# Keys of 16 heads from one dense fp32 projection, in a prologue with another order

## The chip, the cores and the metric

The kernel runs on one core of one Trainium2 chip. The metric is the device time of one execution in microseconds (us). The core's engines are TensorE (PE in the rows, its weight loads PEld), VectorE (DVE), ScalarE (ACT), GpSimd (POOL) and SyncE (SP), which issues all loads and stores.

## What is computed

x is 4 batches of 256 tokens of 128 numbers, and ctx is a context of the same shape. Four layers follow each other; each is a cross-attention to ctx and then a mixture of experts, both gated by tanh and both on normalised x:

```python
for L in range(4):
    x = x + tanh(g_xattn[L]) * xattn[L](layernorm(x), ctx)
    x = x + tanh(g_ffn[L]) * moe[L](layernorm(x))
```

Layer 0's attention is an autocorrelation: the spectra of projected queries and keys are multiplied, the inverse transform gives a correlation for each lag, and the five best lags weigh shifted values. Layers 1 and 3 are softmax attention with 16 heads of 8 numbers. Layer 2 has one shared key and value head and a window of 32. The experts of layer 0 are 40 with 6 chosen for a token, of which 8 only pass their input on.

## The kernel before, in words

All of x stays on chip as eight tiles of 128 tokens. Each engine has its own instruction list, written out in order; semaphores tie them together, and an engine that waits holds up all that stands behind in its list. So the order in the code is the order of the work.

The prologue is what comes before the first experts. SyncE issues every load (x, the constants, the context in three layouts, then all weights, then the ring of expert weights). `autocorrelation` on TensorE transforms the context to frequencies (`dft_tokens`, line 583), projects it to keys (`project`, line 591), makes z and vo (lines 604 and 609, the context times the output and value weights), later transforms and projects normalised x, multiplies back (line 624) and mixes vo with the weights of the lags (lines 631 and 635).

Between these steps stand the keys and values of layers 1 to 3, which depend on ctx alone. There are 23 pieces (`chunks`), a piece being one matmul result of 128 x 512; `KV_AT` sets how many stand at each place. A score has to be nearly fp32 accurate, so each number is split into a high part that the fast fp32r format holds and a rest. Keys are stored for it as stacked rows: for each of four heads in a group 8 rows of high part, 8 of the rest, 8 of the high part again, and 2 rows of the constant 1.0 that carry the row maxima. Before, the weights are laid out in this stacked form (`stacked`), so 16 heads need four pieces of 128 columns for each half of the tokens. Each key piece takes

```python
pe.matmul(o, w[:, 0, :], chi[:, c], start=True, stop=False)
pe.matmul(o, w[:, 0, :], clo[:, c], start=False, stop=False)
mm = pe.matmul(o, w[:, 1, :], chi[:, c], start=False, stop=True)
```

on TensorE (lines 558 to 560), two passes on ScalarE with different signs and scales by row (lines 1025 and 1029), and a sum of the two on GpSimd (line 415), which `stage` holds until it is written to a DRAM buffer (`keys`, line 309). Once all keys are written, `stack_keys` reads them back into kz, the buffer of three batches from which attention takes its weights.

kz has to be zero where no rows are written. GpSimd fills all of it (line 503). The arithmetic of the routing (`route`) and of the experts' first weights comes at the prologue's end: `turn_weights` (line 654) waits for VectorE's routing parts.

## Time and profile before

| | |
|---|---|
| median of 3 runs | 725.25 us |
| lowest, highest | 723.22, 726.19 us |
| the profiled execution, its own time | 724.92 us |
| its span in the profile | 723.1 us |
| TensorE busy, share of the span | 637.2 us, 88% |
| VectorE busy | 526.2 us, 73% |
| ScalarE busy | 379.8 us, 53% |
| GpSimd busy | 266.8 us, 37% |
| mean granted clock of TensorE | 0.962 |

The profile gives each instruction's start and duration, and for each idle stretch the instruction that ended it. Busy shares are means over the whole span; the prologue is its first 100 us. An fp32 matmul stands in the profile as two records, an fp32r matmul as one. The granted clock is 1.00 at 2.4 GHz and 0.50 at 1.2 GHz.

### The profile page before, as it was taken

To read this page: it belongs to the slowest core of one execution; us is meant where nothing else is said; L and a number is where in the kernel's file an instruction comes from. 1 tells how busy PE (TensorE), PEld (TensorE's weight loads), DVE (VectorE), ACT (ScalarE), POOL (GpSimd) and SP (SyncE) were. 2 spreads that over 40 slices of the span, in tenths; PEclk is the share of its full clock that TensorE was granted. 3 is DMA by queue.
4 is the path that set the end of the run, shared out by engine and by line. 5 is a ranking of instruction groups with operands and counts; after the bars stand their busy time and mean duration, and the time that the engine had idled before them with its cause. 6 is when DMAs were issued, how large, how long until landed. Compare 5 with 4: busy or idle time off the path is not lost.

```text
span 723.1 us, 11826 instructions
## 1 busy us (share of the span) xinstructions
PE 637.2 (88%) x3590; PEld 450.3 (62%) x3590; DVE 526.2 (73%) x1290; ACT 379.8 (53%) x652; POOL 266.8 (37%) x463
## 2 busy tenths in 40 slices
PE   2787669998899988998899889999998899987997
PEld 1576537775567655676566546777766677654774
DVE  5473789898787636887864568888877888555886
ACT  1545255543356662543466337777744466632774
POOL 7633355662310121463112115666642100201663
PEclk9998689998999998999999999999999999998999
DMA  8221042111001010011000301111110010000110
GB/s 292 76 90 67 7 152 83 44 40 45 5 3 32 3 32 0 23 44 31 10 5 5 88 0 39 36 44 43 37 37 0 4 33 2 4 1 0 38 44 38
DMA packets 24087, 28.50 MB, mean 39 GB/s; under 512 B 4002, under 2 KB 19938, under 8 KB 24036
## 3 DMA queue, kind: packets, MB, share of 16 engines
q1 hardware_dynamic: 24036, 27.87, 12.3%
q8 instruction: 26, 0.43, 0.2%
q14 instruction: 25, 0.20, 0.1%
HBM read 22.22 MB, written 5.24 MB: 38 GB/s over the span
## 4 chain that ended last, share of the span: by engine, by line
PE 72%; DVE 16%; ACT 5%; issue 4%; POOL 1%; DMA 1%; DVEq 0%; SPq 0%; ACTq 0%; POOLq 0%
PE PS L665 11%; PE PS L666 11%; PE PS L667 11%; PE PS L687 5%; PE PS L891 4%; PE PS L529 4%; PE PS L800 4%; PE PS L874 3%; DVE negmax L1527 2%; DVE consts L1533 2%; PE PS L906 2%; DVE qst L1487 2%; PE PS L871 1%; PE PS L583 1%; PE PS L847 1%
## 5 line engine op out<-in xcount | busy, mean ns | idle before, releaser
L425 POOL TENSOR_TENSOR wpair<-ring,ones_col 128x128 fp32r<-128x128 f32 (+1 forms) x150 | 75.6, 504 | 139.9 <-PE PS L667 96.2
L1432 DVE TENSOR_TENSOR pT<-pT,PS 128x512 f32<-128x512 f32 x150 | 102.4, 684 | 29.3 <-ACT pT L1067 23.5
L1166 ACT ACTIVATE pT<-PS 128x512 f32<-128x512 f32 x160 | 92.0, 592 | 50.1 <-PE PS L874 40.7
L1438 DVE TENSOR_TENSOR hid_lo<-pT,hid_hi 128x512 fp32r<-128x512 f32 x150 | 110.6, 738 | 2.8 <-ACT hid_hi L1074 1.6
L427 POOL TENSOR_TENSOR wpair<-ring,wpair 128x128 fp32r<-128x128 f32 (+1 forms) x150 | 103.2, 688 | 11.7
L1074 ACT ACTIVATE hid_hi<-pT 128x512 fp32r<-128x512 f32 x150 | 93.9, 626 | 14.4 <-DVE pT L1432 13.3
L665 PE MATMUL PS<-hid_hi,wpair 128*128 128x512 f32 x150 | 86.6, 577 | 4.4 <-DVE hid_lo L1438 4.4
L665 PE MATMUL PS<-xhi,wpair 128*128 128x512 f32 x204 | 85.0, 417 | 2.2 <-DVE pT L1432 1.4
L1067 ACT ACTIVATE pT<-PS,ring 128x512 f32<-128x512 f32 x96 | 66.0, 689 | 37.1 <-PE PS L667 37.1
L666 PE MATMUL PS<-xlo,wpair 128*128 128x512 f32 x204 | 82.5, 404 | 0.0
L667 PE MATMUL PS<-xhi,wpair 128*128 128x512 f32 x204 | 82.2, 403 | 0.0
L800 PE MATMUL PS<-kz,qst 128*128 128x256 f32 x256 | 59.0, 314 | 11.5 <-DVE negmax L1533 7.1
L482 POOL CAST nmpart<-negmax 128x8 fp32r<-128x8 f32 x48 | 9.2, 191 | 158.6 <-DVE emask L1540 69.0
L874 PE MATMUL PS<-qst,kz 128*128 128x256 f32 x256 | 65.3, 340 | 2.1 <-ACT pT L1166 2.0
L1533 DVE CUSTOM_DVE_ANT_0 consts<-PS,ctx_tok,negfloor 128x256 bf16<-128x256 f32 x128 | 54.3, 480 | 9.1 <-PE PS L800 8.7
L666 PE MATMUL PS<-hid_lo,wpair 128*128 128x512 f32 x150 | 59.1, 394 | 0.0
L667 PE MATMUL PS<-hid_hi,wpair 128*128 128x512 f32 x150 | 59.1, 394 | 0.0
L1067 ACT ACTIVATE pT<-PS 128x512 f32<-128x512 f32 x54 | 32.0, 597 | 48.9 <-PE PS L667 48.8
L800 PEld LDWEIGHTS PS<-kz,qst 128*128 128x128 f32 x256 | 39.5, 191 | 27.3 <-issue 8.4
L1527 DVE TENSOR_REDUCE negmax<-PS 128x2 f32<-128x512 f32 x64 | 42.8, 689 | 12.5 <-PE PS L800 12.5
L665 PEld LDWEIGHTS PS<-xhi,wpair 128*128 128x128 f32 x204 | 40.2, 197 | 14.4 <-issue 5.0
L874 PEld LDWEIGHTS PS<-qst,kz 128*128 128x128 f32 x256 | 44.7, 194 | 6.9 <-ACT pT L1166 3.0
(242 smaller groups left out, 1252.8 us busy)
## 6 DMA issues: line engine op xcount, KB each, us to landing
ring<-in_mlp SPq DMA_DIRECT2D x48, 128.5 KB, 2.1
ring<-in_glu SPq DMA_DIRECT2D x27, 192.0 KB, 2.4
keys<-qst SPq DMA_DIRECT2D x18, 256.0 KB, 2.0
kz<-keys SPq DMA_DIRECT2D x36, 128.0 KB, 3.1
qst<-kfull SPq DMA_DIRECT2D x96, 4.0 KB
wq<-in_wq SPq DMA_DIRECT2D x3, 256.0 KB, 4.2
consts<-in_consts SPq DMA_DIRECT2D x1, 740.0 KB, 5.0
x_res<-in_x SPq DMA_DIRECT2D x1, 512.0 KB, 3.6
```

The source lines that it names most:

```text
L425: pool.tensor_tensor(wpair[:, pair, 0, c], w, ones, ALU.mult).then_inc(M["wstep"], 1)
L427: pool.tensor_tensor(wpair[:, pair, 1, c], ring[:, slot, c], wpair[:, pair, 0, c].bitcast(f32), ALU.subtract).then_inc(ready, 1)
L665: pe.matmul(o, w_hi, hi, start=start, stop=False, skip_group_check=True)
L666: pe.matmul(o, w_hi, lo, start=False, stop=False, skip_group_check=True)
L667: return pe.matmul(o, w_lo, hi, start=False, stop=start, skip_group_check=True)
L800: mm = pe.matmul(PS[:, v % 2, q * S:(q + 1) * S], qst[:, h // HGRP, b * S + q * P:b * S + (q + 1) * P], keys_of(b, h), start=True, stop=True)
L874: mm = pe.matmul(PS[:, 2 + w % 2, k * S:(k + 1) * S], keys_of(b, h)[:, k * P:(k + 1) * P], qst[:, h // HGRP, b * S:(b + 1) * S], start=(L ...
L1067: act.activation(act_out[:, hf, :], PS[:, 2 + hf, :], func, bias=bias).then_inc(M["act"], 1)
L1074: act.activation(hid_hi[:, kept, :], hid[:, hf, :], ACT.Copy).then_inc(M["hi"], 1)
L1166: act.activation(pT[:, w % 8, :], PS[:, 2 + w % 2, :], ACT.Exp, scale=sc).then_inc(A["p"], 1)
L1432: dve.tensor_tensor(hid[:, hf, :], src[:, hf, :], PS[:, 6 + hf, :], ALU.mult).then_inc(M["hid"], 1)
L1438: dve.tensor_tensor(hid_lo[:, kept, :], hid[:, kept % 2, :], hid_hi[:, kept, :].bitcast(f32), ALU.subtract).then_inc(M["lo"], 1)
```

## The change

The key weights are no longer stacked. A key piece is one fp32 matmul of 128 dense columns, all 16 heads at once (`key_columns` sets their order), for half of the tokens. ScalarE reads the result once and rounds it to fp32r, which is the high part (`key_high`). TensorE then subtracts this high part from the same PSUM bank with a matmul by minus the identity (`key_rest`), and ScalarE reads the rest (`key_low`). Three whole parts per layer are written to DRAM (high, rest, high), and the stacking happens when they are read back, 24 rows instead of 32. The rows of the constant 1.0 are written once, by four small transfers from `ones2` (`flag_keys`). There are 11 pieces instead of 23. GpSimd no longer splits weights or context or sums keys.

The prologue is written in another order. TensorE starts with 14 matmuls on zeros and transforms context and normalised x one behind the other; the correlation follows product by product. VectorE prepares the routing tables ahead of the products. z, vo and layer 1's keys come behind the correlation, the values of layers 1 and 3 behind the mixing, the keys of layers 3 and 2 and layer 2's values behind the first expert's matmuls. The loads come in another order: 640 columns of the constants ahead of ctx_tok, the rest of them later, ctx_nat and ctxT after the small ones. The fill of kz is divided: GpSimd and VectorE fill half of the first batch's place each, ScalarE the other two in eight instructions.

```diff
-        KV_AT = (4, 8, 12, 18)
-        chunks = ([("k", 1, hf, a) for hf in range(NHALF) for a in range(HGRP)]
-                  + [("v", L, hf, 0) for L in (1, 3) for hf in range(NHALF)]
-                  + [("k", 2, hf, 0) for hf in range(NHALF)] + [("v", 2, 0, 0)]
-                  + [("k", 3, hf, a) for hf in range(NHALF) for a in range(HGRP)])
+        chunks = ([("k", 1, 0), ("k", 1, 1)] + [("v", L, hf) for L in (1, 3) for hf in range(NHALF)]
+                  + [("k", 3, 0), ("k", 3, 1), ("k", 2, 0), ("k", 2, 1), ("v", 2, 0)])
+        KV_MIX, KV_LN = 2, 6
...
-            sp.dma_start(consts[:, 0:C_BAND], t["consts"]).then_inc(ld_const, 16)
+            sp.dma_start(consts[:, 0:C_INV], t["consts"][:, 0:C_INV]).then_inc(ld_const, 16)
             sp.dma_start(ctx_tok[:, :, :], t["ctx_tok"]).then_inc(ld_ctx, 16)
...
+            def save_keys(L):
+                sp.wait_ge(kv_out, keys_done[L])
+                for part, rows in enumerate((key_hi[L], key_lo[L], key_hi[L])):
+                    sp.dma_start(kd[L][part, :, :], rows.bitcast(f32)).then_inc(k_saved[L], 16)
...
                     for j in range(HGRP):
-                        rows = slice(32 * j, 32 * j + 32)
+                        rows = slice(32 * j, 32 * j + SROWS)
...
-            pool.memset(kz[:, :, :, :].bitcast(f32), 0.0).then_inc(kz_set, 1)
+            pool.memset(kz[:, 0, 0:H // 2, :].bitcast(f32), 0.0).then_inc(kz_set, 1)
...
                 if kind == "k":
-                    pe.matmul(o, w[:, 0, :], chi[:, c], start=True, stop=False)
-                    pe.matmul(o, w[:, 0, :], clo[:, c], start=False, stop=False)
-                    mm = pe.matmul(o, w[:, 1, :], chi[:, c], start=False, stop=True)
+                    mm = pe.matmul(o[0:wk[L].shape[1], :], wk[L][:, :], ctxT[:, hf * HALF:(hf + 1) * HALF], start=True,
+                                   stop=False, skip_group_check=True)
...
+            def key_rest(n):
+                kind, L, hf = chunks[n]
+                rows = wk[L].shape[1]
+                pe.wait_ge(kv_hi, k_before[n] + 1)
+                pe.matmul(PS[0:rows, 6 + n % 2, :], minus[0:rows, 0:rows], key_hi[L][:, hf * HALF:(hf + 1) * HALF],
+                          start=False, stop=True, skip_group_check=True).then_inc(kv_rest, 1)
...
-                    for c in range(KV_AT[3], len(chunks)):
-                        key_value(c)
+                    for c in (KV_LN, KV_LN + 2):
+                        for half in (c, c + 1):
+                            key_value(half)
+                        for half in (c, c + 1):
+                            key_rest(half)
+                    key_value(len(chunks) - 1)
...
-            pe.wait_ge(set_pool, 3)
-            pe.wait_ge(set_dve, 2)
+            pe.wait_ge(set_pool, 1)
+            keep_busy(7, 14)
             autocorrelation()
...
+            def key_high(n):
+                act.activation(key_hi[L][:, hf * HALF:(hf + 1) * HALF], PS[0:rows, 6 + n % 2, :], ACT.Identity,
+                               bias=consts[0:rows, col:col + 1]).then_inc(kv_hi, 1)
+            def key_low(n):
+                act.wait_ge(kv_rest, k_before[n] + 1)
+                act.activation(key_lo[L][:, hf * HALF:(hf + 1) * HALF], PS[0:rows, 6 + n % 2, :], ACT.Identity,
+                               bias=consts[0:rows, col:col + 1]).then_inc(kv_out, 1)
...
+            def zero_keys(first, last):
+                for c in range(first, last):
+                    act.activation(blocks[:, c, :, :], zerob[:, :].unsqueeze(1).broadcast_to([P, 2, HALF]),
+                                   ACT.Copy).then_inc(kz_set, 1)
...
             def autocorrelation():
+                dve.memset(kz[:, 0, H // 2:H, :].bitcast(f32), 0.0).then_inc(kz_set, 1)
...
+                prepare_routing()
+                for n, (qx, kx) in enumerate(((0, 0), (0, 1), (1, 1), (1, 0))):
+                    dve.wait_ge(ac["kfe"], kx + 1)
+                    dve.wait_ge(ac["qfreq"], qx + 1)
+                    dve.tensor_tensor(prod[:, (0, 3, 1, 2)[n], :], PS[:, 6 + qx, :], kfreq[:, kx, :], ALU.mult).then_inc(ac["prod"], 1)
...
-                prepare_routing()
```

TensorE's list at the kernel's start, before. PS is PSUM, consts the constants with the transform matrix, att_w the weights of layer 0, oT the buffer of z and vo, qst the split context:

```order
L583 MATMUL PS<-consts,ctx_tok 128x256 [waits ld_const,ld_ctx,set_dve,set_pool]
L583 MATMUL PS<-consts,ctx_tok 128x256 x7
L591 MATMUL PS<-att_w,kf 128x128 [waits ld_att0,ac_kine]
L591 MATMUL PS<-att_w,kf 128x128 x7
L604 MATMUL PS<-att_w,kfull 128x128 [waits ld_ctx]
L604 MATMUL PS<-att_w,kfull 128x128 x7
L609 MATMUL PS<-oT,att_w 128x512 [waits ac_ze]
L609 MATMUL PS<-oT,att_w 128x512
L558 MATMUL PS<-qst,hid_hi 128x512 [waits ac_voe,wk_split1,bias_rows,ctx_lo]
...
L583 MATMUL PS<-consts,xn 128x256 [waits ln_xn]
L583 MATMUL PS<-consts,xn 128x256 x7
L591 MATMUL PS<-att_w,kf 128x128 [waits ac_qine]
```

And in the changed kernel, where zerob is a tile of zeros, kf the context's spectrum and oT that of x:

```order
L508 MATMUL PS<-zerob 128x512 [waits set_pool]
L508 MATMUL PS<-zerob 128x512 x13
L567 MATMUL PS<-consts,ctx_tok 128x256 [waits ld_ctx,ld_const]
L567 MATMUL PS<-consts,ctx_tok 128x256 x7
L567 MATMUL PS<-consts,xn 128x256 [waits ln_xn]
L567 MATMUL PS<-consts,xn 128x256 x3
L567 MATMUL PS<-consts,xn 128x256 [waits ln_xn]
L567 MATMUL PS<-consts,xn 128x256 x3
L575 MATMUL PS<-att_w,kf 128x128 [waits ac_kine,ld_att0]
L575 MATMUL PS<-att_w,kf 128x128 x7
L575 MATMUL PS<-att_w,oT 128x128 [waits ac_qine]
```

The transform of x (`xn`) stood behind two projections, vo and four key pieces; it now stands right behind the context's, and the wait for VectorE's constants (`set_dve`) is gone from the first.

VectorE's list before, from its first instructions and around the products of the spectra (line 1302; pT<-PS,qf), with the routing tables (wrpair, b2part) behind them:

```order
L1564 CAST identb<-consts 128x128 [waits ld_const]
L1566 CAST pick<-consts 96x32
...
L1297 COPY kf<-PS 128x512 [waits ac_qin]
L1302 TENSOR_TENSOR pT<-PS,qf 128x512 [waits ac_qfreq,ac_kfe]
L1302 TENSOR_TENSOR pT<-PS,qf 128x512 x3
L1304 TENSOR_TENSOR pT<-pT 128x512 [waits ac_prod]
L1283 CAST wrpair<-wr 128x40 [waits ld_route]
...
L1290 TENSOR_TENSOR b2part<-pT,b2part 96x128 [waits dstep]
L1309 MAX pT<-PS 128x8 [waits ac_corr,dstep]
```

And in the changed kernel:

```order
L1308 MEMSET kz 128x2048
L1248 BN_STATS stats<-x_res 128x6 [waits ld_x]
...
L1325 COPY oT<-PS 128x512 [waits ac_qin]
L1298 CAST wrpair<-wr 128x40 [waits ld_route,bias_rows]
...
L1305 TENSOR_TENSOR b2part<-pT,b2part 96x128 [waits dstep]
L1332 TENSOR_TENSOR pT<-PS,qf 128x512 [waits ac_qfreq,ac_kfe,dstep]
L1332 TENSOR_TENSOR pT<-PS,qf 128x512 [waits ac_qfreq,ac_kfe] x3
L1334 TENSOR_TENSOR pT<-pT 128x512 [waits ac_prod]
L1338 MAX pT<-PS 128x8 [waits ac_corr]
```

The tables stand ahead of the products now, the casts of the constants behind the normalisation (not shown), and each maximum waits for its own batch.

ScalarE's list before, around z and vo (oT) and around the exponential of the lag weights (pT, 128x20):

```order
L1184 ACTIVATE oT<-PS 128x1024 [waits ac_z]
L1186 ACTIVATE oT<-PS 128x1024 [waits ac_vo]
L1188 ACTIVATE gtan<-gates 128x8 [waits ld_gate]
L1025 ACTIVATE qst<-PS,kbs,consts 128x512 [waits vall_set,set_dve,kv_mm]
L1029 ACTIVATE kfull<-PS,kba,consts 128x512
...
L1035 ACTIVATE vall<-PS 128x64x8 [waits kv_mm] x4
L1040 ACTIVATE qf<-pick 96x2048 [waits ac_prod]
L1198 ACTIVATE pT<-pT 128x20 [waits ac_top]
L1025 ACTIVATE qst<-PS,kbs,consts 128x512 [waits k_saved0,kv_mm]
L1029 ACTIVATE kfull<-PS,kba,consts 128x512 [waits k_ready]
```

And in the changed kernel, from the context's projected spectrum (qf) on:

```order
L1195 ACTIVATE qf<-PS 128x512 [waits ac_kfreq] x2
L1197 ACTIVATE oT<-PS 128x1024 [waits ac_z]
L1017 ACTIVATE qst<-PS,consts 128x512 [waits kv_mm,ld_rest]
L1017 ACTIVATE qst<-PS,consts 128x512 [waits kv_mm]
L1202 ACTIVATE pT<-pT 128x20 [waits ac_top]
L1204 ACTIVATE oT<-PS 128x1024 [waits ac_vo]
L1025 ACTIVATE qst<-PS,consts 128x512 [waits kv_rest] x2
L1208 ACTIVATE pT<-PS 128x512 [waits ac_mo]
L1036 ACTIVATE vall<-PS 128x64x8 [waits kv_mm,vall_set]
```

The exponential stood behind the four value pieces and the spreading of picks; it now stands behind the copy of z and two high key parts, which wait for TensorE's key matmuls.

## Rows read from the trace of the kernel before

**Rows 1.** The profile's page, busy time, share of the span and instructions.

```profile
...
PE 637.2 (88%) x3590; PEld 450.3 (62%) x3590; DVE 526.2 (73%) x1290; ACT 379.8 (53%) x652; POOL 266.8 (37%) x463
...
```

**Rows 2.** Chain of waits, 0 to 45 us: start, us, engine, tile and line.

```profile
...
6.34 7.43 DVE pick L1566
...
13.86 6.62 PE PS L583 x16
...
```

**Rows 3.** DMA issues, 0 to 100 us: KB each, us from issue to landing.

```profile
...
ring<-in_glu SPq DMA_DIRECT2D x4, 192.0 KB, 4.7
...
x_res<-in_x SPq DMA_DIRECT2D x1, 512.0 KB, 3.6
ctx_tok<-in_ctx_tok SPq DMA_DIRECT2D x1, 512.0 KB, 5.8
...
kz<-keys SPq DMA_DIRECT2D x1, 128.0 KB, 3.0
...
```

**Rows 4.** SyncE issues in order of time: start, us, how many.

```profile
...
15.76 1.85 SPq L333 DMA_DIRECT2D ring<-in_glu  x4
...
```

**Rows 5.** TensorE in order of time: start, us, line, operation, records.

```profile
...
21.31 2.05 PE L591 MATMUL PS<-att_w,kf 128*128 128x128 f32 x16 [0.85 <-DVE kf L1294]
...
26.26 1.98 PE L609 MATMUL PS<-oT,att_w 128*128 128x512 f32 x4 [1.11 <-ACT oT L1184]
...
45.01 5.34 PE L624 MATMUL PS<-consts,pT 128*128 128x256 f32 x24
...
58.77 5.26 PE L563 MATMUL PS<-wv,ctxT 128*128 128x8 f32 x32 [2.27 <-ACT kfull L1029]
...
70.26 1.99 PE L635 MATMUL PS<-oT,pT 128*128 128x256 f32 x8 [1.59 <-ACT pT L1202]
77.97 2.27 PE L541 MATMUL PS<-consts,xn 128*128 128x128 f32 x8 [5.72 <-DVE xn L1242]
...
83.97 0.77 PE L665 MATMUL PS<-xhi,wpair 128*128 128x512 f32 x1
...
88.69 0.40 PE L558 MATMUL PS<-qst,hid_hi 128*128 128x512 f32 x1
...
```

**Rows 6.** TensorE and others by stretch: busy, then granted clock (PEclk).

```profile
...
80.00:84.00 4.00, 3.68 (x19) 3.47 (x17) 1.11 (x2) 0.60 (x1) 2.69 (x5) 0.50 0.00 0
88.00:95.00 7.00, 5.16 (x19) 2.96 (x17) 6.68 (x31) 5.66 (x11) 3.83 (x3) 1.00 0.14 52
...
```

**Rows 7.** ScalarE in order of time.

```profile
...
25.19 1.02 ACT L1184 ACTIVATE oT<-PS 128x1024 f32<-128x1024 f32 x1 [0.70 <-PE PS L604]
...
41.37 0.78 ACT L1025 ACTIVATE qst<-PS,kbs,consts 128x512 fp32r<-128x512 f32 x1 [2.94 <-PE PS L560]
...
```

**Rows 8.** VectorE in order of time.

```profile
...
40.74 2.48 DVE L1302 TENSOR_TENSOR pT<-PS,qf 128x512 f32<-128x512 f32 x4 [2.21 <-PE PS L591]
...
44.65 2.58 DVE L1283 CAST wrpair<-wr 128x40 fp32r<-128x40 f32 x4
...
51.03 0.43 DVE L1309 MAX8 pT<-PS 128x8 f32<-128x256 f32 x1
...
72.36 0.75 DVE L1276 SCALAR_TENSOR_TENSOR x_res<-PS,gtan,x_res 128x512 f32<-128x512 f32 x1 [10.47 <-PE PS L635]
...
84.18 0.49 DVE L1345 COPY pT<-PS 128x320 f32<-128x320 f32 x1 [2.57 <-PE PS L648]
...
91.16 1.59 DVE L1374 SCALAR_TENSOR_TENSOR pT<-pT 128x320 f32<-128x320 f32 x1
...
98.67 0.90 DVE L1403 TENSOR_TENSOR pT<-pT 128x256 bf16<-128x256 f32 x1
...
```

**Rows 9.** GpSimd (POOL) in order of time.

```profile
...
3.26 10.40 POOL L503 MEMSET kz<- 128x12288 f32 x1
...
42.90 5.46 POOL L415 TENSOR_TENSOR qst<-qst,kfull 128x512 fp32r<-128x512 f32 x4 [5.54 <-ACT kfull L1029]
...
91.12 6.62 POOL L415 TENSOR_TENSOR qst<-qst,kfull 128x512 fp32r<-128x512 f32 x5 [8.28 <-ACT kfull L1029]
...
```

More of the change, by code:

```diff
@@ L131, in build @@
         kz = sb("kz", [P, KSLOTS, H, S], f32r)
-        kd = {L: nc.dram_tensor(f"keys{L}", (P, 1 if L == 2 else HGRP, N), f32, kind="Internal").ap() for L in range(1, 4)}
+        kd = {L: nc.dram_tensor(f"keys{L}", (3, HD if L == 2 else P, N), f32, kind="Internal").ap() for L in range(1, 4)}
         v_cols = {1: NT * H * 9, 2: B * NW * 9, 3: NT * H * 9}
@@ L406, in layer_norm @@
                     pool.tensor_tensor(rstd[:, c], veps[:, c], mhalf[:, c], ALU.pow).then_inc(ln_rstd, 1)
-            def complete_keys(first, last):
-                for n in range(first, last):
-                    kind, L, hf, a = chunks[n]
-                    if kind == "k":
-                        k = k_before[n]
-                        pool.wait_ge(kv_out, n + 1)
-                        pool.tensor_tensor(stage(k), stage(k).bitcast(f32), kfull[:, k % 2, :], ALU.add).then_inc(k_ready, 1)
             def split_weights(L, glu):
@@ L636, in autocorrelation @@
                                    vo[:, b * S:(b + 1) * S], start=True, stop=True)
-                mm.then_inc(ac["out"], 1)
+                    if b % 2 == 1:
+                        mm.then_inc(ac["out"], 1)
+                for n in range(KV_MIX, KV_LN):
+                    key_value(n)
             def route(L, hf):
@@ L1201, in _ @@
+            for n in range(0, KV_MIX):
+                key_low(n)
             act.wait_ge(ac["mo"], 1)
-            act.activation(mixo, PS[:, 2, :], ACT.Copy).then_inc(ac["moe"], 1)
+            act.activation(mixo, PS[:, 0, :], ACT.Copy).then_inc(ac["moe"], 1)
+            act.wait_ge(vall_set, 6)
+            for n in range(KV_MIX, KV_LN):
+                values(n)
             layer_norm(1)
+            spread_picks()
             route(0)
-            for n in range(KV_AT[3], len(chunks)):
-                key_value(n)
+            for c in (KV_LN, KV_LN + 2):
+                for n in (c, c + 1):
+                    key_high(n)
+                for n in (c, c + 1):
+                    key_low(n)
@@ L1207, in _ @@
+            values(len(chunks) - 1)
             experts(0, True)
@@ L1258, in layer_norm @@
                         ln_statistics(s, 0)
[L1259 removed]
+                if s > 0:
                     ln_apply(s, 0)
@@ L1486, in finish_queries @@
                     dve.wait_ge(A["qt"], pre["qt"] + HGRP * hf + a + 1)
-                    dve.scalar_tensor_tensor(out=dst, in0=PS[:, bank, :], scalar=consts[:, C_SGN + 3:C_SGN + 4],
+                    dve.scalar_tensor_tensor(out=dst, in0=PS[:, bank, :], scalar=consts[:, C_SGN + 1:C_SGN + 2],
                                              in1=dst.bitcast(f32), op0=ALU.mult, op1=ALU.add).then_inc(A["qe"], 1)
```

351 lines of the change are left out of this document (163 added, 188 removed).

## The prediction, before the changed kernel was run

> **What bounds the kernel now.** I read the profile's page first: TensorE is busy 88% of the span [rows 1], but that is a mean over four layers and a prologue. The change touches the prologue alone, up to where the first mixture of experts has its routing weights, so I read the chain of waits from 0 us on, and then each engine in order of time there. Seen so, the prologue is a chain of waits rather than of TensorE work, and it ends at 99.6 us (98.67 + 0.90) [rows 8]. Four things make it long.
>
> First, GpSimd's zero fill of kz holds from 3.26 to 13.66 us [rows 9]. VectorE's casts of the constants, issued at 6.3, end at 13.77 [rows 2], just behind it, although consts was there. TensorE waits for them and starts at 13.86. Second, that first transform takes 6.62 us for 16 records of 256 columns, 0.41 each [rows 2]; later the same shape takes 5.34 us for 24, 0.22 each [rows 5]: the first ran at the lower of TensorE's two levels, 1.2 GHz. Third, keys are made in 18 pieces, each with two ScalarE passes (0.78 us, the second 0.67 behind the first) [rows 7] and a GpSimd sum; the query transform, the value pieces and the mixing matmuls stand behind them in the queues. That is why the products of the spectra start at 40.74 and the result is added to x only at 72.36, after 10.47 us in which VectorE idled [rows 8]. Fourth, GpSimd's sums (5.46 us for four, 6.62 for five) [rows 9] lie beside VectorE's small casts and routing arithmetic, which are slow there: four casts of at most 40 columns take 2.58 us, one pass over 320 elements 1.59 [rows 8].
>
> **The new order, step by step.** Times are those of the changed kernel, worked out from the rows.
>
> *Start.* SyncE issues one load per 0.46 us (four in 1.85) [rows 4]. x lands at 4.3, as before (issue 0.7 + 3.6) [rows 3]. ctx_tok landed 5.8 us after its issue at 1.7, behind 740 KB of consts; only 320 KB of it stand ahead now. Between x's landing and its own lay 1,252 KB in 3.1 us, 400 KB per us, so 420 KB less is 1.1 us: it lands at 6.4. But 14 zero matmuls stand ahead of it from 1.3 us on: 0.43 us each at 1.2 GHz (512 columns), 6.0 in all. TensorE starts its first transform at 7.3, not 13.86: 6.5 us gained. I let the clock rise at about 8.5, since in rows 2 it needed all of 6.6 us of work. So the first transform takes 4.1 us (three records at 0.41, 13 at 0.22) and ends at 11.4. x must be normalised by then; from the add at 72.36 to the first transposes at 77.97 [rows 5, 8] such a normalisation takes 5.6 us even with two adds in it, so it is ready by 9.9. Query transform 3.6: 15.0. Then both projections, 2.05 each [rows 5]: 17.1 and 19.1, the first half of the second at 18.1.
>
> *VectorE before the products.* It copies the query spectrum at 15.0 to 15.7 and then prepares the routing tables, which stood behind the products and stand ahead of them now. Before, this took 6.4 us (44.65 to 51.03) [rows 8], the first 3.7 under GpSimd's sums (to 48.36) [rows 9]. GpSimd is now idle until the expert weights land (15.76 + 4.7 = 20.5) [rows 3, 4], so I take 3.2: the uncovered 2.7, and an estimate of 0.5 for the small casts that GpSimd held up. If that cover fails, 3.2 more. Products start at 18.9 instead of 40.74.
>
> *Products to add.* Four products take 2.48 [rows 8]. The twelve correlation matmuls (0.445 each) [rows 5] now follow product by product, so batch 0 is done 4.7 us after the products' start and batch 3 at 6.0. Maxima take 1.0 us a batch (0.43 for the values [rows 8], as much for their places, and a load): 8.7. VectorE then has 0.9 of lag work. ScalarE's exponential stands behind the copy of z (1.02) [rows 7] and two key copies: z's matmuls end at 8.0, the two key matmuls (0.99 each, fp32 of 512 columns) [rows 5] at 10.0, the second copy at 10.8, the exponential at 11.0, so VectorE waits 1.4 us. This is the late thing that comes next. Weights and mixing matrix take 2.1 (13.1), transposes 0.6 (13.7); ScalarE is at the copies of vo and the two low key parts until 14.4, then copies the mixing matrix, 15.0; half of the last product (1.99 for both) [rows 5], 16.0. The add starts at 18.9 + 16.1 = 35.0 instead of 72.36: 37.4 gained. The rest of TensorE's old work here, four value pieces, now lies in the gap in which it idled 5.72 us [rows 5].
>
> *Add to logits.* 11.8 us before (72.36 to 84.18) [rows 8]. The halves are now chained one behind the other; by the same durations I get 11.3, logits at 46.3.
>
> *Routing.* VectorE needed 15.4 us (84.18 to 99.57); without GpSimd's 6.62 us of sums [rows 9] I get 9.8, since the last eight instructions took 8.4 there (91.16 to 99.57) and should take some 2.8, by the 0.49 of an undisturbed pass over 320 elements at 84.18 [rows 8]. But TensorE must get through 12 expert matmuls and all keys of layers 3 and 2 before it turns the weights, and each pair of key halves now goes matmul, ScalarE, matmul, ScalarE, with the bank free only then. At 2.4 GHz: expert matmuls 2.9, keys of layer 3 until 7.1, of layer 2 until 9.95 (its value piece may start), the 32 small records 5.26 as before [rows 5]: 15.2. So this becomes the bound here, and the turn comes at 46.3 + 15.2 = 61.5 instead of 99.6. VectorE's gain of 5 us is lost again.
>
> The sum: 99.6 - 61.5 = 38.1 us. The profiled execution took 724.92 us, so 686.8; the median is 0.3 above it, so 687.
>
> **What I take as nothing.** The zero fill on VectorE (2,048 columns; GpSimd took 0.85 ns per column [rows 9]) lies ahead of x's landing if it runs at once. If GpSimd's fills hold VectorE as they did in rows 2, it ends near 7.3 and moves the products by 1.1. The Trainium skill ("SBUF — State Buffer", Who interferes with whom) says that the port shared by VectorE and GpSimd is held for the whole instruction, and that a VectorE instruction with at most one SBUF input outside the two-port modes does not contend; for the casts the trace agrees (7.43 us behind the fill), for a memset nothing here shows it. By the Trainium skill the term is 0, by the row 1.1.
>
> ScalarE's eight fills of 1,024 columns (1.02 each by [rows 7]) lie in gaps: four before the first spectrum, two and two between copies whose next wait is longer. The ones written by DMA, the keys' way through DRAM (9 saves instead of 18) and the restacking have no reader before layer 1's attention, over 80 us later. Restacking the last batch there and in layer 3 moves 24 rows instead of 32, landing 3.0 before [rows 3]. Layers 1 to 3 otherwise issue the same work.
>
> The Trainium skill ("DMA: Bandwidth & Descriptors", Why a DMA increments its semaphore by 16 and not by 1) speaks against that edit: a transfer is spread over the largest number up to 16 that divides its slowest dimension, so 32 rows use 16 engines and 24 use 12. Its runs of 1 KB are 8 per engine either way, and by that rule the price is 0 too. No row before has 24 rows.
>
> **Rivals.** (1) *The key chain at the lower clock*, 0.14. From 80 to 84 us TensorE was granted half [rows 6], having idled 5.72 us [rows 5], and twelve matmuls from 83.97 to 88.69 took 4.7; after 88 it had full clock. Half clock through the whole chain gives 5.1 + 5.5 + 5.6 + 5.8, about 22 us instead of 15.2: 694. Against it: the value pieces fill that idle stretch now. (2) *TensorE never warms early*, 0.04: every TensorE step up to the add at half rate costs some 16 us more: 703. (3) *The start does not move*, because a load that the first transform needs is late and the order of loads buys nothing; TensorE starts at 13.9 again: 6.6 less gain, 693.5, 0.04. (4) *More than forecast*, 0.05: the clock rises by 6, key halves overlap, the small records at full rate (4.0): 683. (5) *Slower than before*, 0.03: restacking of the last batch in layers 1 and 3. Each must be late by more than 19 us, half of the 38.1, before it decides; at 21 each the kernel is 3.6 slower, 729. That needs a transfer seven times its 3.0 us; nothing speaks for that but the new shape.
>
> **How the numbers follow.** The forecast has 0.70. Its own bounds: -1.2 (small records at full rate), -0.9 (clock), +1.1 (fill), +3.2 (routing tables uncovered), +2.5 (first transforms cold): 684 to 693. With rivals 1, 3 and 4, which hold 0.23, the range is 681 to 697; outside lie rivals 2 and 5 and tails of the rest. A measurement of this kernel can tell about 0.5%, 3.6 us. All but rival 5 and a mishap I don't see are over 28 us off, so 0.95 faster, 0.02 within, 0.03 slower.
>
> **What will show it.** The first transform starts near 7.3 with ctx_tok landed before; the products near 18.9; VectorE waits 1.4 us for ScalarE's exponential; the add at 35; logits at 46; the turn of the weights waits for TensorE's small records and not for VectorE; the routing passes that took 1.59 and 0.90 take under 0.6; from there on all stages are as long as before. Wrong I am if the products wait for the tables by more than 4 us, if the clock is at half past 46, or if layers 1 to 3 change their length.

## The result, and the profile after

The changed kernel takes 689.44 us (median of 4 runs, 687.98 to 691.10); the kernel before took 725.72 on the same chip (4 runs, 723.22 to 727.65). The ratio is 0.950, with a 95% interval of 0.946 to 0.954: 36 us, or 5%, less. The forecast was 687 (681 to 697). The profiled execution took 688.41 us, with a span of 686.6 where before had 723.1.

The milestones of the forecast come first, in the order of time on TensorE and VectorE of the changed kernel (start, us, engine, line, operation, count; in brackets the wait ahead of it). TensorE:

```profile
1.31 6.00 PE L508 MATMUL PS<-zerob 128*128 128x512 bf16 x14 [1.31 <-POOL ones_col L393]
8.02 3.69 PE L567 MATMUL PS<-consts,ctx_tok 128*128 128x256 f32 x16 [0.71 <-DMA ctx_tok<-in_ctx_tok]
11.55 3.62 PE L567 MATMUL PS<-consts,xn 128*128 128x256 f32 x16
...
46.73 0.77 PE L657 MATMUL PS<-xhi,wpair 128*128 128x512 f32 x1
...
51.72 1.88 PE L531 MATMUL PS<-ctxT,wk 128*128 128x512 f32 x4
...
58.18 3.88 PE L535 MATMUL PS<-wv,ctxT 128*128 128x8 f32 x32 [0.18 <-ACT kfull L1025]
61.91 1.07 PE L646 MATMUL PS<-identb,pT 128*96 128x128 bf16 x8
```

VectorE of the same kernel:

```profile
1.23 1.76 DVE L1308 MEMSET kz<- 128x2048 f32 x1 [1.23 <-PEq L1722]
...
15.89 0.42 DVE L1298 CAST wrpair<-wr 128x40 fp32r<-128x40 f32 x4
...
19.17 2.48 DVE L1332 TENSOR_TENSOR pT<-PS,qf 128x512 f32<-128x512 f32 x4
...
24.17 0.43 DVE L1338 MAX8 pT<-PS 128x8 f32<-128x256 f32 x1 [1.34 <-PE PS L596]
...
29.86 0.17 DVE L1351 TENSOR_REDUCE pT<-pT 128x4 f32<-128x20 f32 x1 [0.78 <-ACT pT L1202]
...
34.66 0.75 DVE L1291 SCALAR_TENSOR_TENSOR x_res<-PS,gtan,x_res 128x512 f32<-128x512 f32 x1 [2.64 <-PE PS L624]
...
46.94 0.49 DVE L1373 COPY pT<-PS 128x320 f32<-128x320 f32 x1 [1.99 <-PE PS L640]
...
53.92 0.77 DVE L1402 SCALAR_TENSOR_TENSOR pT<-pT 128x320 f32<-128x320 f32 x1
...
56.69 0.42 DVE L1431 TENSOR_TENSOR pT<-pT 128x256 bf16<-128x256 f32 x1
63.01 0.42 DVE L1436 COPY pT<-PS 96x512 bf16<-96x512 bf16 x1 [5.90 <-PE PS L646]
```

Read against [rows 2], the first transform starts 5.8 us earlier and takes 3.69 instead of 6.62. Against [rows 8], the products start at 19.17 instead of 40.74, the add at 34.66 instead of 72.36, the logits at 46.94 instead of 84.18. The last routing pass over 256 elements ends at 57.1 instead of 99.6, and from there VectorE waits 5.90 us: TensorE turns the weights at 61.91, behind 32 small records, and is now the later of the two.

The second view is the table by stretch of the same kernel (stretch, length, busy time of PE, PEld, DVE, ACT, POOL, then the granted clock, DMA share and GB/s):

```profile
42.00:46.00 4.00, 2.59 (x17) 2.26 (x17) 1.57 (x5) 2.37 (x2) 0.00 (x0) 0.82 0.78 155
46.00:50.00 4.00, 4.00 (x13) 3.32 (x13) 2.42 (x5) 0.97 (x3) 0.00 (x0) 0.50 0.00 0
50.00:55.00 5.00, 4.55 (x13) 2.34 (x12) 4.69 (x31) 3.05 (x6) 2.15 (x4) 0.86 0.00 0
```

From 46 to 50 TensorE had half clock (1.2 GHz) although it was busy all the time; it had idled 1.55 and 1.41 us ahead of the two routing steps. The second routing step already ran slower: from its first to its last matmul record 1.51 us pass (45.01 to 46.52), in the first step 0.77 (41.91 to 42.68). The twelve expert matmuls run from 46.73 to 51.72.

### The profile page after: what moved, and what is told of

Read it like the earlier page. It is cut to its first block, busy times and chain, and to the rows that moved or that the text cites. A ratio compares the mean times of both kernels' runs of the same rounds, so it can differ in the third digit from the quotient of the medians.

```text
span 686.6 us, 11700 instructions
## 1 busy us (share of the span) xinstructions
PE 627.4 (91%) x3547; PEld 440.9 (64%) x3571; DVE 506.5 (74%) x1287; ACT 368.6 (54%) x635; POOL 227.3 (33%) x438
## 4 chain that ended last, share of the span: by engine, by line
PE 75%; DVE 15%; ACT 4%; issue 3%; DMA 1%; POOL 1%; DVEq 0%; SPq 0%; ACTq 0%
PE PS L657 12%; PE PS L659 12%; PE PS L658 11%; PE PS L679 5%; PE PS L889 4%; PE PS L798 4%; PE PS L508 4%; PE PS L872 3%; DVE negmax L1555 2%; DVE consts L1561 2%; PE PS L904 2%; DVE qst L1515 2%; PE PS L869 1%; DVE pT L1460 1%; DVE hid_lo L1466 1%
## 5 line engine op out<-in xcount | busy, mean ns | idle before, releaser
L411 POOL TENSOR_TENSOR wpair<-ring,ones_col 128x128 fp32r<-128x128 f32 (+1 forms) x150 | 78.4, 523 | 171.6 <-PE PS L659 115.0
L413 POOL TENSOR_TENSOR wpair<-ring,wpair 128x128 fp32r<-128x128 f32 (+1 forms) x150 | 99.6, 664 | 11.8
L657 PE MATMUL PS<-xhi,wpair 128*128 128x512 f32 x204 | 85.6, 419 | 2.0 <-DVE pT L1460 1.7
L659 PE MATMUL PS<-xhi,wpair 128*128 128x512 f32 x204 | 83.3, 408 | 0.0
L508 PE MATMUL PS<-zerob 128*128 128x512 bf16 x181 | 50.0, 421 | 2.7 <-POOL ones_col L393 1.3
```

The costliest lines, as they stand in the source:

```text
L411: pool.tensor_tensor(wpair[:, pair, 0, c], w, ones, ALU.mult).then_inc(M["wstep"], 1)
L413: pool.tensor_tensor(wpair[:, pair, 1, c], ring[:, slot, c], wpair[:, pair, 0, c].bitcast(f32), ALU.subtract).then_inc(ready, 1)
L657: pe.matmul(o, w_hi, hi, start=start, stop=False, skip_group_check=True)
L659: return pe.matmul(o, w_lo, hi, start=False, stop=start, skip_group_check=True)
```

## The experiments

Unless a text says otherwise, "the turn" is the start of TensorE's transposes of the routing weights (61.91 in the changed kernel), where the changed part ends. e1 to e4, e6 and e7 are one run each, read by the milestones of their profile; e5 and e8 to e11 were timed in 4 to 6 runs. The milestones say more than a single total: from the turn to the end of the span, where the code hardly differs, the traces took between 622.2 us (e8) and 626.2 (e10), e5 apart.

**What the start is worth: e1, e2, e3.** Three kernels, each with one part of the new start undone. e1 leaves out the zero matmuls:

```diff
-            keep_busy(7, 14)
```

> The changed kernel without the 14 zero matmuls ahead of the first transform; all else as it is. In the changed kernel the first transform starts at 8.02 us and takes 3.69 us for 16 records, and the products of the spectra start at 19.17. Theory (the zero matmuls are what brings TensorE to 2.4 GHz before the context lands): the first transform starts at about 7.9 and takes 6.6 us, as in the kernel before; the second is at full rate; everything behind is 3 us later, so the products start at 22.2 and the span grows from 686.6 to about 689.6. Rival (the clock rises with time or with the loads, or VectorE's tables hide the loss): the first transform takes 3.7 to 4.5 us and the products start at 19.2 to 19.6.

Measured: 688.41 us (before on that chip 723.88), TensorE's first rows being

```profile
7.81 5.22 PE L567 MATMUL PS<-consts,ctx_tok 128*128 128x256 f32 x16 [7.81 <-DMA ctx_tok<-in_ctx_tok]
12.87 3.62 PE L567 MATMUL PS<-consts,xn 128*128 128x256 f32 x16
```

The cold first transform costs 1.5 us more (not the 3 expected), the products start 1.2 later, the turn comes at 63.20, 1.3 later, and the total does not show it. So the zero matmuls buy 1.3 us at the turn. The band load, which costs other traces up to 2 us (below), was not waited for here. e2 gives the whole zero fill back to GpSimd:

```diff
-            pool.memset(kz[:, 0, 0:H // 2, :].bitcast(f32), 0.0).then_inc(kz_set, 1)
+            pool.memset(kz[:, :, :, :].bitcast(f32), 0.0).then_inc(kz_set, 10)
-            zero_keys(0, 4)
...
-                dve.memset(kz[:, 0, H // 2:H, :].bitcast(f32), 0.0).then_inc(kz_set, 1)
```

> The changed kernel with the whole zero fill of kz on GpSimd again, as one instruction at its old place; VectorE and ScalarE fill nothing. The fill takes 10.4 us by the kernel before, so 3.4 to 13.8. Theory (what costs is GpSimd's place in the normalisation): the reciprocal roots stand behind the fill, x is normalised at 16 us instead of 8.3, the second transform starts at 16 instead of 11.55, VectorE's copies and tables follow, and the products start at 24.7 instead of 19.17: 5.5 us, and the span grows to about 692. Rival (the fill had cost only because VectorE's casts waited behind it, and these now stand later): the products start before 20.5 and the span stays within 1.3 us.

Measured: 696.28 us, span 694.5, turn at 72.12. VectorE of e2 during the fill (GpSimd's memset runs there from 3.43 to 13.77), and the steps that follow:

```profile
5.65 8.14 DVE L1247 TENSOR_SCALAR veps<-mv 128x4 f32<-128x4 f32 x1
5.73 8.06 DVE L1244 BATCH_NORM_STATS2 stats<-x_res 128x6 f32<-128x128 f32 x4
...
14.98 2.14 DVE L1252 TENSOR_SCALAR xn<-x_res,mv,rstd 128x128 f32<-128x128 f32 x8 [0.48 <-POOL rstd L401]
...
22.20 1.25 DVE L1294 CAST wrpair<-wr 128x40 fp32r<-128x40 f32 x4
```

and its TensorE:

```profile
16.15 5.40 PE L567 MATMUL PS<-consts,xn 128*128 128x256 f32 x16 [4.36 <-DVE xn L1252]
...
28.47 7.11 PE L596 MATMUL PS<-consts,pT 128*128 128x256 f32 x24 [3.35 <-DVE pT L1327]
```

One pass over four columns lasts 8.14 us: it ends where GpSimd's memset ends. Then TensorE, idle for 4.36 us, does the second transform at the lower clock (5.40 instead of 3.62), and the tables slide beside GpSimd's work on the expert weights (the four casts 1.25 instead of 0.42), so the products start at 27.63, 8.5 us later instead of the 5.5 expected. After 3.35 us more of idle time the correlation matmuls take 7.11 us instead of 5.42. That is 10.2 us at the turn, more than either expectation. The Trainium skill ("SBUF — State Buffer", Who interferes with whom) says that a pass in a two-port mode blocks fully while GpSimd holds the shared port; the trace agrees with the length of the wait, 8.14 us for what takes 0.17 elsewhere; the mode of an instruction is not in its rows.

e3 puts the loads back as they stood, the whole of the constants ahead of ctx_tok and the other context loads right behind it:

```diff
+            sp.dma_start(consts[:, C_INV:C_BAND], t["consts"][:, C_INV:]).then_inc(ld_rest, 16)
...
+            sp.dma_start(ctx_nat[:, :, :], t["ctx_nat"]).then_inc(ld_nat, 16)
+            sp.dma_start(ctxT[:, :], t["ctxT"]).then_inc(ld_ctxT, 16)
...
-            sp.dma_start(consts[:, C_INV:C_BAND], t["consts"][:, C_INV:]).then_inc(ld_rest, 16)
```

> The changed kernel with the loads at the head of the queue in the order of the kernel before: all of the constants (still in two transfers) ahead of ctx_tok, and ctx_nat and ctxT right behind it, ahead of the layer 0 weights and the small loads. In the changed kernel ctx_tok landed 6.2 us after its issue at 1.65, at 7.9, and the first transform waits for it; my prediction had 6.4. Theory A (transfers land in the order of their bytes, 400 KB per us, as I had it): ctx_tok lands 1.0 us later, at 8.9, and the span is 1 us longer. Theory B (transfers issued behind it share the engines, and narrow rows slow all of them, so that the order ahead of it decides little): ctx_tok lands at 7.3 to 8.1 and the span stays within 0.7 us, or the layer 0 weights become what is late.

Measured: 690.14 us, span 688.3:

```profile
1.31 5.28 PE L508 MATMUL PS<-zerob 128*128 128x512 bf16 x14 [1.31 <-POOL ones_col L393]
8.82 5.38 PE L567 MATMUL PS<-consts,ctx_tok 128*128 128x256 f32 x16 [2.23 <-DMA ctx_tok<-in_ctx_tok]
```

ctx_tok comes 0.8 us later, as theory A had it; but its load is also issued 0.5 later, behind one more, so that only 0.4 are left from issue to landing (6.6 us instead of 6.2). After 2.23 us of idle time the transform takes 1.7 more. 2.4 us at the turn. The order of loads is worth little by itself; it matters because the zero matmuls must reach near to the data: in the eight other traces with zero matmuls the gap was 0.3 to 1.7 us and the transform took 3.69. That the longer gap is the cause rests on this one trace.

**The tables' place: e4.** `prepare_routing()` goes back behind the four products and their subtraction:

```diff
-                prepare_routing()
                 for n, (qx, kx) in enumerate(((0, 0), (0, 1), (1, 1), (1, 0))):
...
+                prepare_routing()
```

> The changed kernel with VectorE's routing tables behind the five products, where they stood before, instead of ahead of them. Theory (both places cost about the same because the correlation matmuls leave VectorE 1.3 us only): products start at 17.8 instead of 19.17, the tables take 3.3 us behind them and end at 24.7, so the first maximum starts at 24.7 instead of 24.17, the add at 35.2 instead of 34.66, the span is 0.5 us longer. Rival 1 (GpSimd splits the first expert weights from 20.9 to 25 us and holds VectorE's small casts, as its sums did before): the tables take 5 to 6.5 us and the add comes at 37 to 38, the span 3 us longer. Rival 2 (ahead of the products they cost their full length): the span is 1.4 us shorter.

Measured: 693.03 us, span 691.2. VectorE of e4:

```profile
18.08 2.48 DVE L1331 TENSOR_TENSOR pT<-PS,qf 128x512 f32<-128x512 f32 x4 [2.08 <-PE PS L575]
...
21.21 0.41 DVE L1298 CAST wrpair<-wr 128x40 fp32r<-128x40 f32 x4
21.66 1.45 DVE L1299 TENSOR_TENSOR wrpair<-wr,wrpair 128x40 fp32r<-128x40 f32 x4
...
26.91 0.43 DVE L1338 MAX8 pT<-PS 128x8 f32<-128x256 f32 x1 [0.21 <-DVE b2part L1305]
```

The products start 1.1 us sooner, but the tables now take 5.5 us instead of 3.2, beside GpSimd's splits of the expert weights that begin at 21.64, and the maxima wait for the tables: 2.7 us later. This is rival 1, and a little more: TensorE idles 4.03 us until the mixing matrix is there and then mixes the lags at the lower clock (0.50 granted from 34 to 38 us):

```profile
36.25 3.47 PE L624 MATMUL PS<-oT,pT 128*128 128x256 f32 x8
```

That is 3.47 us instead of 1.99, so the add comes at 38.27, 3.6 later, and the turn 3.8. The place ahead of the products is the better one because it lies in front of GpSimd's work.

**Is it the order alone? e5, e8, e9.** e5 is the kernel before with all 23 key and value pieces behind the first expert's matmuls, the old form of the keys kept and all else in its old order:

```diff
-        KV_AT = (4, 8, 12, 18)
+        KV_AT = (0, 0, 0, 0)
```

> The kernel before with the 23 key and value pieces in their old form (stacked weights, three matmuls, two ScalarE passes, a GpSimd sum), but all of them moved behind the first expert's matmuls: order without the dense form. Theory (the order alone does not pay, the pieces only move to the other wait, where 15.4 us are free): add at about 57 instead of 72.4, logits at 69, but 23 pieces of 1.33 us or more behind the first expert's matmuls, so that the turn of the weights comes at 106 to 110 instead of 99.6 and the kernel takes 732 to 736 us, slower than 725. Rival (moving the pieces out of the queue ahead of the add is most of the gain): the kernel takes 700 to 712 us.

Measured: 739.67 us (738.48 to 741.85), ratio 1.021 (1.018 to 1.025), slower than the 732 to 736 expected. The add comes at 59.32, 13 us sooner than before, but the turn at 109.36, 10 later. With the keys in 18 pieces, what the add gains is more than lost behind it: to have all keys and values late, without the dense form, makes the kernel slower. The rest of the new order (x's transform early, tables ahead) and a smaller number of late pieces were not tried with the old form.

e8 is the kernel before with the fill divided over three engines and nothing else:

```diff
-            pool.memset(kz[:, :, :, :].bitcast(f32), 0.0).then_inc(kz_set, 1)
+            pool.memset(kz[:, 0, 0:H // 2, :].bitcast(f32), 0.0).then_inc(kz_set, 1)
...
+            act.wait_ge(set_pool, 3)
+            zero_keys(0, 6)
...
+            dve.memset(kz[:, 0, H // 2:H, :].bitcast(f32), 0.0).then_inc(kz_set, 1)
```

> The kernel before with only the zero fill of kz divided as in the changed kernel (GpSimd and VectorE half of the first place each, ScalarE eight instructions, six ahead of its first copy and two behind the mixing matrix). Theory (the fill held VectorE's casts and so TensorE's start, and the start is on the path all the way): the casts end at 6.5, the first transform starts at about 8.9, when ctx_nat has landed, instead of 13.86, and everything behind is 5 us earlier: 720 us. Rival (the start is hidden, since the key weights are split on GpSimd later anyway): the kernel stays within 1.5 us of 725.

Measured: 720.46 us (719.25 to 721.26), ratio 0.994 (0.992 to 0.997). TensorE's start, its mixing matmuls and its arrival at the turn:

```profile
8.93 6.11 PE L583 MATMUL PS<-consts,ctx_tok 128*128 128x256 f32 x16 [8.93 <-DMA kfull<-in_ctx_nat]
...
65.78 3.78 PE L635 MATMUL PS<-oT,pT 128*128 128x256 f32 x8 [1.17 <-ACT pT L1211]
...
96.26 1.09 PE L654 MATMUL PS<-identb,pT 128*96 128x128 bf16 x8 [4.13 <-DVE pT L1413]
```

The start comes 4.9 us sooner, the products 5.4 (35.32), the add 2.7 (69.67), the turn 3.4. About half of the gain is lost before the add: VectorE idles 13.19 us ahead of it, where it idled 10.47 [rows 8]. Two thirds of that loss are clock: the granted clock is 0.50 from 58 to 70 us, and the mixing matmuls take 3.78 us instead of 1.99 [rows 5].

e9 is the changed kernel with its work in about the order of the kernel before: context first, all values and keys ahead of the mixing.

```diff
                 project(dft_k, 4, W[:, P:2 * P], ac["kfreq"])
...
+                for n in range(0, KV_MIX):
+                    key_rest(n)
+                for hf in range(NHALF):
+                    pe.wait_ge(ln_xn, 4 * hf + 4)
+                    dft_tokens(xn, 2, hf, ac["qin"])
...
+                for c in (KV_LN, KV_LN + 2):
+                    for half in (c, c + 1):
+                        key_value(half)
+                    for half in (c, c + 1):
+                        key_rest(half)
+                key_value(len(chunks) - 1)
```

> The changed kernel with the dense keys, its loads, its fills and its zero matmuls, but the steps in about the order of the kernel before: context transform and projection, z and vo, layer 1's keys, then x's transform, the products, the correlation, then all other key and value pieces, and only then the mixing of the lags and the add. Theory (the dense form shortens the pieces, but in the queue ahead of the add each still costs its full length; the order is worth another 11 us or so): add at about 51 instead of 34.7, logits at 63, the turn of the weights then waits for VectorE and comes at 73 instead of 61.9, the kernel takes 698 to 705 us. Rival (the dense form is nearly all of the gain): below 693.

Measured: 704.31 us (702.52 to 706.61), ratio 0.974 (0.971 to 0.976), inside the theory's range, though the add (54.71), the logits (68.12) and the turn come 3.7 to 5.1 us later than it had them. TensorE's turn waits for VectorE there, as it did before:

```profile
78.06 1.09 PE L653 MATMUL PS<-identb,pT 128*96 128x128 bf16 x8 [5.66 <-DVE pT L1431]
```

So with the old order, the dense form, the fill and the new start give 19.6 us of the 34.8 that the changed kernel had on this chip (723.94 to 689.19); the order gives the other 15.

**Is TensorE's chain the bound up to the turn? e6, e7, e10.** e6 does the 32 small value records of layer 2 twice over (the same products into the same place):

```diff
-                    for i in range(B * NW):
+                    for i in list(range(B * NW)) * 2:
```

> The changed kernel with the 16 small matmuls of layer 2's values done twice (the same results written again). In the changed kernel they take 3.9 us, and VectorE idles 5.9 us until the weights are turned. Theory (TensorE's key chain ends the prologue): all behind is 3.7 to 4.0 us later, the turn at 65.7 instead of 61.9, span about 690.4. Rival (VectorE's routing or another wait ends it, with slack): less than 1 us.

Measured: 698.92 us, span 697.1. TensorE, and the granted clock by stretch:

```profile
60.00 11.71 PE L535 MATMUL PS<-wv,ctxT 128*128 128x8 f32 x64 [0.17 <-ACT kfull L1025]
71.57 1.07 PE L646 MATMUL PS<-identb,pT 128*96 128x128 bf16 x8
```

```profile
60.00:65.00 5.00, 5.00 (x34) 5.00 (x34) 0.00 (x0) 0.55 (x1) 0.00 (x0) 0.73 0.92 293
65.00:70.00 5.00, 5.00 (x25) 5.00 (x25) 0.00 (x0) 0.00 (x0) 0.00 (x0) 0.50 0.09 33
```

The 7.8 us that the records grow by are all in the turn. The chain is the bound. The other 1.8 us by which the turn is late come from the front: VectorE's tables waited 1.98 us for the band load, TensorE idled 3.26 us, and the correlation matmuls behind took 7.00 us instead of 5.42; part of this was won back at the twelve expert matmuls (4.07 us instead of 4.99). The doubled records did not take twice 3.88, for the clock fell to half while they ran.

e7 puts five zero matmuls in each of the two gaps of 1.4 to 1.6 us ahead of the routing logits:

```diff
             layer_norm(1, (0,))
+            keep_busy(5, 5)
             route(0, 0)
             layer_norm(1, (1,))
+            keep_busy(5, 5)
             route(0, 1)
```

> The changed kernel with five zero matmuls (1.1 us at full clock) in each of the two gaps in which TensorE waits for VectorE's xlo (40.4 to 41.9 and 43.6 to 45.0 us). In the changed kernel the granted clock falls to 0.50 in 42 to 46 and the first expert's twelve matmuls take 5.0 us. Theory (the idle stretches let the clock fall): the clock stays at 1.00 until the keys, the twelve matmuls take 2.9, the turn comes 2 us earlier and the span is about 684.5. Rival (the clock falls anyway, because the routing and transpose matmuls are too narrow to count as work, or the fillers only push the chain): turn within 0.5 us of 61.9 or later.

Measured: 689.90 us, span 688.1. TensorE of e7:

```profile
46.87 0.49 PE L657 MATMUL PS<-xhi,wpair 128*128 128x512 f32 x1
...
49.73 1.88 PE L531 MATMUL PS<-ctxT,wk 128*128 128x512 f32 x4
...
56.27 6.09 PE L535 MATMUL PS<-wv,ctxT 128*128 128x8 f32 x32 [0.18 <-ACT kfull L1027]
```

The twelve matmuls take 2.86 us, not 4.99: with the gaps filled the clock stayed up here, as the theory says. But the small records now take 6.09 us instead of 3.88, at a granted clock of 0.50 from 58 us on, and the turn, 62.21, is about where it was (its products started 0.9 us later, for the band load): the clock fell anyway, only later. Beside e11 below, whose products start nearly as late (19.88; here 20.11), the turn is 0.8 us sooner, not 2.

e10 takes work off that chain instead. Layer 3's keys go into the two gaps; layer 2's small records do not share a bank with the keys and do not wait for them; the exponential and the copy of the mixing matrix go ahead of ScalarE's key copies; the tables no longer wait for the band load, which they do not read.

```diff
+            key_value(KV_LN)
             route(0, 0)
             layer_norm(1, (1,))
+            key_value(KV_LN + 1)
+            key_rest(KV_LN)
             route(0, 1)
+            key_rest(KV_LN + 1)
...
-                o = PS[:, 6 + n % 2, :]
+                o = PS[:, 6 + n % 2, :] if (kind, L) != ("v", 2) else PS[:, 0, 384:512]
...
+            act.activation(cw[:, 1, :], cw[:, 0, :], ACT.Exp).then_inc(ac["exp"], 1)
+            for n in range(0, KV_MIX):
+                key_high(n)
```

> The changed kernel with four edits that shorten what the profile shows as late: the band load no longer counts among those the routing tables wait for; ScalarE's exponential stands ahead of the high key parts, and its copy of the mixing matrix ahead of the low ones; layer 3's two key matmuls stand in the two gaps in which TensorE waits for xlo; layer 2's small value matmuls go to free columns of another PSUM bank, ahead of the rests, so that they wait for no ScalarE copy. Theory: the add comes 1.4 us earlier (33.3), logits at 45.5, the clock stays up through the first expert's matmuls, and the weights are turned when VectorE is done, 10.2 to 10.8 us behind the logits instead of 15: about 56, and the kernel takes 682 to 684 us where the changed kernel takes 688.5 to 690. Rival 1 (the small matmuls lower the clock wherever they stand): turn 12 to 13 us behind the logits, 685 to 686. Rival 2 (the keys in the gaps delay the logits): no faster than the changed kernel.

Measured: 680.91 us (679.22 to 683.68), ratio 0.939 (0.938 to 0.941). TensorE of e10, and the clock of the stretch that had 0.50 in the changed kernel:

```profile
45.09 0.40 PE L657 MATMUL PS<-xhi,wpair 128*128 128x512 f32 x1
...
47.95 1.88 PE L531 MATMUL PS<-ctxT,wk 128*8 128x512 f32 x4
49.77 3.74 PE L535 MATMUL PS<-wv,ctxT 128*128 128x8 f32 x32
...
55.73 1.06 PE L646 MATMUL PS<-identb,pT 128*96 128x128 bf16 x8 [1.66 <-DVE pT L1442]
```

```profile
46.00:50.00 4.00, 4.00 (x15) 1.83 (x14) 3.30 (x6) 3.71 (x7) 1.75 (x3) 1.00 0.57 224
```

The turn comes 10.8 us behind the logits (44.97) where it took 15.0, and TensorE waits for VectorE again. This is the fastest version of the study, 1 us below the range of the theory: 8.3 us less than the changed kernel on the same chip (e11), 43 less than before. Beside e11's milestones, 1.9 us are won up to the add (33.52; 35.37), 1.2 from there to the logits and 4.3 from the logits to the turn. Its four edits were not separated.

**The changed kernel once more: e11**, beside e9 and e10 on their chip, without an edit.

> The changed kernel itself, for comparison on the same chip: 688 to 690 us. In two runs the routing tables waited 1.1 and 2.0 us for the band load; where that happens the products of the spectra start at 20 to 20.8 us instead of 19.17 and the add comes 1 to 3 us later.

Measured: 689.19 us (687.26 to 692.13), ratio 0.953 (0.950 to 0.955). Its VectorE shows a wait that the first profile did not have:

```profile
16.60 0.42 DVE L1298 CAST wrpair<-wr 128x40 fp32r<-128x40 f32 x4 [0.98 <-DMA band<-in_band]
```

and its small records take longer:

```profile
58.41 4.78 PE L535 MATMUL PS<-wv,ctxT 128*128 128x8 f32 x32 [0.18 <-ACT kfull L1025]
```

The turn comes at 63.04. So the same program gives 4.15 us for the twelve expert matmuls and 4.78 for the small records in one trace, 4.99 and 3.88 in the other: single terms of this part move by about 1 us without any edit.

## Why the prediction was right, point by point

**Start.** Predicted 7.3 and 4.1 us; measured 8.02 and 3.69, the sum being 0.3 off. Two terms were mis-sized and cancelled. ctx_tok does not land at 6.4 but at 7.9, 6.2 us after its issue, and it is this load that the transform waits for, not the zero matmuls: one of the signs that I named, ctx_tok landed before, failed. I credited 420 KB less ahead of it with 1.1 us, and it came 0.4 later than before (5.8 from issue to landing). That credit is not borne out: the same list of loads gave 5.4 to 6.3 us in other traces (e9, e2), and e3, with the bytes ahead again, gave 6.6. What a load issued behind does to it no run told apart. On the other side the clock was up at the first record, not after three; e1 and e3, where it was not, took 5.22 and 5.38. Rivals 2 and 3 did not happen.

**Zero fill on VectorE.** I took 0 and kept 1.1 as the bound. The memset ran from 1.23 to 2.99 beside GpSimd's fills, and nothing behind it was held up: 0. The Trainium skill's rule ("SBUF — State Buffer", Who interferes with whom) that a VectorE instruction with at most one SBUF input outside the two-port modes does not contend with GpSimd was the right one here (1.76 us for 2,048 columns; GpSimd's own fill of as many took 1.81), and [rows 2] the wrong neighbour. What was under-priced was the other side: I put the fill at 6.5 us of start. By e2 it is worth 10.2 at the turn in the new order, by e8 3.4 in the old one. The price of one edit depends on what stands behind it.

**Tables and products.** Predicted 3.2 us and 18.9; measured 3.24 and 19.17. e4 shows the cover that I named failing, at 5.5 us. The band load is the part I had left out: the tables' wait includes it, and it was 0 us in the changed kernel's first profile, 0.98 in e11, 1.12 in e7 and 1.98 in e6.

**Products to logits.** Predicted 35.0 and 46.3; measured 34.66 and 46.94. VectorE waited 0.78 us for the exponential instead of 1.4: its own work was done 9.9 us behind the products' start (I had 9.6) and the exponential at 10.6 (11.0), since the two dense key matmuls take 0.94 each rather than 0.99 and the two copies 1.48 together. e10, with the exponential ahead of the key copies, has no wait there. From the add to the logits I had 11.3 us and it took 12.28, more than the 11.8 of before: the second routing step ran at the lower clock, 1.51 us from its first to its last record instead of 0.77. In e10, where the clock stayed up, it is 11.45.

**Routing, to the turn.** Predicted 15.2 us behind the logits, measured 14.97. This is the step with the largest terms that were wrong, and that it came out within 0.3 us is luck. The twelve matmuls took 4.99 us where I had 2.9: rival 1, half clock, came true for these twelve, since the value pieces fill one idle stretch but leave 1.55 and 1.41 us just ahead of the logits. The clock was back by 51.7, so the keys did not run at half, and they took less than I had (6.46 us from 51.72 to the small records; I had 7.05). The small records held the chain for 3.73 us, not 5.26 [rows 5]: those of before (58.77 to 64.03) ran into a stretch where the clock fell, as its own table shows:

```profile
60.00:65.00 5.00, 5.00 (x26) 4.81 (x26) 1.89 (x4) 0.33 (x2) 1.48 (x2) 0.57 0.28 105
```

Full rate for them was one of my bounds. It would not have been a sure value either: in the other traces of kernels with dense keys the 32 records took 3.74 (e10) to 6.09 us (e7), and 4.78 in e11, the same kernel. An error of +2.1 met -0.6, -1.5 and the 0.2 by which the matmuls started ahead of the copy. VectorE's side was as described: done by 57.1, 10.2 us behind the logits (I had 9.8), the passes of [rows 8] now 0.77 and 0.42 instead of 1.59 and 0.90; only the first misses "under 0.6".

**From the turn on.** 38.1 predicted at the turn, 37.7 measured. I took the rest as equal; of the 37.7, 1.2 us went in layer 0's experts. The normalisation that ends them starts, before and after, at:

```profile
181.19 1.02 POOL L406 TENSOR_TENSOR rstd<-veps,mhalf 128x4 f32<-128x4 f32 x1 [3.21 <-DVE veps L1237]
```

```profile
144.69 1.01 POOL L401 TENSOR_TENSOR rstd<-veps,mhalf 128x4 f32<-128x4 f32 x1 [3.27 <-DVE veps L1251]
```

The difference there is 36.5, and 36.5 at the end of the span. The stretch from the turn to there took 81.57 before and 82.78 after, but in e11, the same kernel, 81.59 (63.04 to 144.63), and 81.2 to 82.8 in the others. So the 1.2 us are not the change's; what makes a run take the one or the other is open. The restacking of the last batch, rival 5, cost nothing that the profile shows; it was not tried alone.

Two of my sums are slightly off: at 21 us each, rival 5 makes the kernel 3.9 us slower and not 3.6, and my own bounds around 687 add up to 685 to 694, not 684 to 693.

Divided up, on the chip of e9 and e10: the fill about 3 of the 35 us (e8, on another chip), dense form and start some 16, not separated, the order 15. e5 shows that the late place of the keys and values loses time in the old form; that no other order would pay with it is not shown.

## What to carry to other kernels

Price a prologue as a chain, engine by engine, and ask at each join which of two arrivals is later: the same fill was worth 3 us in the old order and 10 in the new. Moving work later pays only if it fits where it goes: all 23 old pieces moved late made the kernel slower, the 11 with dense keys did not. Then the bound came to be the chain of small matmuls and copies, and four edits together, among them real work instead of zeros in TensorE's gaps, took another 8 us off. An idle stretch on TensorE can cost twice, once by its length and once by the clock behind it: in e2, e4 and e6 a step behind an idle stretch of 3.3 to 4.4 us took 1.5 to 1.8 us more. When a forecast hits, check its terms: here most were off by 0.4 to 2.1 us and cancelled.

## What the runs showed of the hardware that was not expected

- After idle gaps of 1.55 and 1.41 us TensorE ran at half clock from 46 to 50 us (changed kernel); with zero matmuls in the gaps the twelve matmuls behind them took 2.86 us instead of 4.99 (e7). The same 24 correlation records took 5.42 us behind an idle gap of 1.27 us, 7.11 behind 3.35 (e2) and 7.00 behind 3.26 (e6).
- TensorE's clock fell during its matmuls of 8 columns or right behind them, sooner in some traces than in others, also of the same kernel: 32 records took 3.7 to 3.9 us where it fell only at their end or behind them (granted 0.91 from 60 to 62 us and 0.50 from 62 in the changed kernel), and 4.1 (e3) to 6.1 us (e7) where it fell earlier; 64 took 11.7, with 0.50 granted at the end although TensorE was busy 5.00 of 5.00 us (e6).
- A load of 512 KB took 6.2 us with 320 KB issued between x and it, and before 5.8 with 740; with the same list it took 5.4 (e9) to 6.3 (e2). The band, the same load in the same place, was waited for by 0 to 1.98 us from one kernel to another, and by 0 and 0.98 in two traces of the same one.
- VectorE's memset of 2,048 columns ran in 1.76 us while GpSimd was filling, but a pass over 4 columns stood for 8.14 us behind the same kind of fill (e2).
